# Two edits in an eight-sequence decoder kernel: output products of the first self attention per pair of sequences' halves, and the tail of the second self attention in another order

## The reference, cut to what matters

```
x = x + L0_attn(layernorm(x))            # 16 heads of 64, relative bias, softmax, then out @ Wo + bo
x = x + L0_xattn(layernorm(x), ctx)      # cross attention
x = x + L0_ffn(layernorm(x))             # 16 gated experts
x = x + L1_attn(layernorm(x))            # below
x = x + L1_xattn(layernorm(x), ctx)
x = x + L1_ffn(layernorm(x))             # 8 experts

# L1_attn(z): attention, then two layer norms with gamma and beta
h   = layer_norm(z + attention(z) @ Wout + bout) * gamma + beta
ffn = relu(h @ W1 + b1) @ W2 + b2
out = layer_norm(h + ffn) * gamma + beta
```

## Time and profile before

| | us |
|---|---|
| median of 3 runs (581.82, 582.07, 584.65) | 582.07 |
| the profiled execution | 586.07 |
| its span, first to last instruction | 584.3 |
| first self attention's loop in it, from the first scores to the last addition to x_all | about 117 |
| tail of the second self attention in it, from L1659 to the last L1671 | 35 |
| PE busy in the span | 482.6 (83%) |
| DVE, ACT, POOL busy | 372.1, 335.4, 264.1 |

### The profile page before, as it was taken

One profiled execution on the slowest core, in us unless ns is written; L12 is line 12 of the kernel. 1 busy time (PEld: TensorE's weight loads), 2 busy tenths in 40 slices (PEclk: granted clock), 3 DMA queues, 4 the chain that ended last, 5 costly groups with the idle time before them and its releaser, 6 DMA issues. The chain is left out here.

```text
span 584.3 us, 10052 instructions
## 1 busy us (share of the span) xinstructions
PE 482.6 (83%) x3221; PEld 370.9 (63%) x3221; DVE 372.1 (64%) x906; ACT 335.4 (57%) x659; POOL 264.1 (45%) x294
## 2 busy tenths in 40 slices
PE   4699999998688858899986995927678687999996
PEld 2578787876466636688853674524456474777774
DVE  4777777764737635466654676377437467788875
ACT  3787676765447745355543452404447465888883
POOL 1799687767335640566643900012001471354410
PEclk9799999999759976999995998877779957999999
DMA  6605332333264000544414000002660001121101
GB/s 190 210 24 151 94 101 84 92 89 101 75 145 121 1 2 2 156 134 130 123 38 121 1 1 0 1 14 69 169 163 1 2 1 37 37 59 51 36 0 36
DMA packets 34689, 41.81 MB, mean 72 GB/s; under 512 B 5178, under 2 KB 26612, under 8 KB 34420
## 3 DMA queue, kind: packets, MB, share of 16 engines
q1 hardware_dynamic: 33796, 40.65, 25.2%
q10 hardware_dynamic: 848, 0.60, 0.4%
HBM read 30.70 MB, written 8.18 MB: 67 GB/s over the span
## 5 line engine op out<-in xcount | busy, mean ns | idle before, releaser
L1251 POOL TENSOR_TENSOR e_gc<-e_g,e_c 128x512 f32<-128x512 f32 x32 | 42.0, 1313 | 42.3 <-ACT e_g L1234 22.4
L1995 DVE TENSOR_TENSOR e_h_lo<-e_h,e_h_hi 128x512 fp32r<-128x512 f32 x60 | 51.0, 881 | 15.1 <-ACT e_h_hi L1856 15.0
L944 ACT ACTIVATE x_pT<-x_turn 77x1024 f32<-77x1024 f32 x32 | 32.6, 1020 | 33.4 <-PE x_turn L890 33.4
L1852 ACT ACTIVATE e_h<-e_h,m_b 128x512 f32<-128x512 f32 x64 | 43.5, 686 | 11.0 <-PE e_h L1754 10.9
L546 ACT ACTIVATE a_p<-xn_all,a_least 128x128 f32<-128x128 f32 x128 | 40.7, 390 | 6.1 <-DVE a_least L578 6.0
L890 PE MATMUL x_turn<-consts,x_p 128*77 128x128 f32 x256 | 40.1, 306 | 4.5 <-ACT x_p L949 4.5
L692 POOL TENSOR_TENSOR a_p<-a_p,a_r 128x512 f32<-128x512 f32 x32 | 33.3, 1040 | 20.1 <-DVE a_r L587 20.1
L890 PEld LDWEIGHTS x_turn<-consts,x_p 128*77 128x77 f32 x256 | 32.0, 165 | 14.2 <-ACT x_p L949 12.1
L1210 ACT ACTIVATE e_h_hi<-e_h 128x512 fp32r<-128x512 f32 x34 | 21.5, 632 | 33.8 <-DVE e_h L1293 28.2
L1299 DVE TENSOR_TENSOR e_h_lo<-e_h,e_h_hi 128x512 fp32r<-128x512 f32 x34 | 23.8, 699 | 26.3 <-ACT e_h_hi L1210 26.3
L575 DVE TENSOR_TENSOR xn_all<-a_score,w_bias 128x256 f32<-128x256 f32 x64 | 24.1, 419 | 23.0 <-PE a_score L445 23.0
(11 more groups left out here) (302 smaller groups left out, 1471.2 us busy)
## 6 DMA issues: line engine op xcount, KB each, us to landing
e_c<-spread SPq DMA_DIRECT2D x32, 256.0 KB, 3.3
x_ks<-kstack SPq DMA_DIRECT2D x16, 462.0 KB, 5.7
kstack<-a_blk_hi SPq DMA_DIRECT2D x32, 154.0 KB, 3.1
m_w<-in_L_ffn_W SPq DMA_DIRECT2D x16, 256.0 KB, 3.0
a_raw<-in_experts SPq DMA_DIRECT2D x17, 192.0 KB, 2.4
kstack<-a_blk_lo SPq DMA_DIRECT2D x16, 154.0 KB, 2.8
su_reversed<-scratch SPq DMA_DIRECT2D x1, 1024.0 KB, 5.9
w_wkv<-in_L_attn_Wkv SPq DMA_DIRECT2D x1, 1024.0 KB, 8.1
```

The lines of the kernel that those rows point to most:

```text
L944: act.activation(pT[k % 2][:, :, :], tb[0:NKV, :, :], ACT.Copy).then_inc(S["turned_out"], 1)
L1251: pool.tensor_tensor(gc[k % 2][:, :], g[u % 2][:, :], c[k % NC][:, :], ALU.mult).then_inc(S["weighted"], 1)
L1852: act.activation(h[half][f], hb[f][:, :], ACT.Gelu, bias=b1[j][:, f:f + 1]).then_inc(S["gelu_done"], 1)
L1995: dve.tensor_tensor(h_lo[half][f][:, :], h[half][f], h_hi[half][f][:, :].bitcast(F32), ALU.subtract).then_inc(S["lo_done"], 1)
```

## The change

In attention0 the output products are made in odd t alone, for both sequences of a pair at once, with the operands the other way round: the weights are stationary and 256 columns (two sequences of 128 positions) move, so the result comes out transposed. After every eighth group ACT copies it to SBUF (yT), PE transposes it back into the other half of the same bank, and DVE adds from there to x_all, one step later than before and at the start of its step. In the second self attention a norm is four statistics, four aggregates and the variance as before, then four instructions (y - mean) * gamma, which don't need POOL's result, then four y * rstd + beta, each with a semaphore of its own for the transposes; in the last norms the addition of x_all takes the place of the one of beta. The separate passes L1652, L1663 and L1671 are gone. PE's order is turn(0), up(0), turn(1), down(0), up(1), down(1).

```diff
-                for n in range(G + OUT):
+                for n in range(G + OUT + 1):
...
+                    t = n - OUT - 1
+                    if 0 <= t < G and t % 8 == 7:
+                        pe.wait_ge(S["yT_out"], t // 8 + 1)
+                        for k in range(2):
+                            mm = pe.transpose(yb[:, 2 + k, :], yT[:, P * k:P * k + P], ident)
+                        mm.then_inc(S["y_turned"], 1)
                     t = n - OUT
-                    if 0 <= t < G:
-                        i, hg, b = t // 8, (t // 2) % 4, t % 2
-                        if t == 0:
+                    if 0 <= t < G and t % 2 == 1:
+                        i, hg = t // 8, (t // 2) % 4
+                        if t == 1:
...
                         for c in (2 * hg, 2 * hg + 1):
-                            mm = pe.matmul(yb[:, b, :], oT[:, b, c, :], wo[:, c, :], start=(c == 0 and b == 0),
-                                           stop=(c == 7 and b == 1))
+                            mm = pe.matmul(yb[:, 0:2, :], wo[:, c, :], oT[:, :, c, :], start=(c == 0), stop=(c == 7))
...
-                for n in range(G + VALUE):
+                for n in range(G + OUT + 1):
+                    t = n - OUT - 1
+                    if 0 <= t < G and t % 8 == 7:
+                        act.wait_ge(S["y_done"], 4 * (t // 8) + 4)
+                        act.activation(yT[:, :], yb[:, 0:2, :].rearrange("p b d -> p (b d)"),
+                                       ACT.Copy).then_inc(S["yT_out"], 1)
...
-                for n in range(G + OUT + 1):
+                for n in range(G + OUT + 2):
+                    t = n - OUT - 2
+                    if 0 <= t < G and t % 8 == 7:
+                        i = t // 8
+                        dve.wait_ge(S["y_turned"], i + 1)
+                        dve.wait_ge(S["bo_added"], 1)
+                        xp = x_all[:, 2 * i:2 * i + 2, :]
+                        dve.tensor_tensor(xp, yb[:, 2:4, :], xp, ALU.add).then_inc(S["x_out"], 1)
...
-                    t = n - OUT - 1
-                    if 0 <= t < G and t % 8 == 7:
-                        i = t // 8
-                        dve.wait_ge(S["y_done"], t + 1)
-                        dve.wait_ge(S["bo_added"], 1)
-                        xp = x_all[:, 2 * i:2 * i + 2, :]
-                        dve.tensor_tensor(xp, yb[:, 0:2, :], xp, ALU.add).then_inc(S["x_out"], 1)
...
-                def norm(k, h):
+                def norm(k, h, dst, add, done):
...
+                    own_values(*[dve.scalar_tensor_tensor(out=y[:, b, :], in0=y[:, b, :], scalar=mv[:, b, 0:1], in1=gamma,
+                                                          op0=ALU.subtract, op1=ALU.mult) for b in of_half])
                     dve.wait_ge(S["rstd_ready"], k + 1)
-                    own_values(*[dve.tensor_scalar(y[:, b, :], y[:, b, :], mv[:, b, 0:1], rstd[:, b:b + 1],
-                                                   ALU.subtract, ALU.mult) for b in of_half])
-                    own_values(dve.tensor_tensor(ys[h], ys[h], free(gamma, [[0, HB], [1, P]]), ALU.mult))
+                    for b in of_half:
+                        dve.scalar_tensor_tensor(out=dst[:, b, :], in0=y[:, b, :], scalar=rstd[:, b:b + 1], in1=add(b),
+                                                 op0=ALU.mult, op1=ALU.add).then_inc(done, 1)
...
-                    norm(h, h)
-                    dve.tensor_tensor(hs[h], ys[h], free(beta, [[0, HB], [1, P]]), ALU.add).then_inc(S["h_ready"], 1)
+                    norm(h, h, hh, lambda b: beta, S["h_ready"])
...
-                    norm(2 + h, h)
-                    own_values(dve.tensor_tensor(xs[h], xs[h], ys[h], ALU.add))
+                    norm(2 + h, h, x_all, lambda b: x_all[:, b, :], S["x_ready"])
```

More of the change, by code:

```diff
@@ L345, in attention0 @@
             oT = sb("oT", [P, 2, 8, P])
+            yT = sb("yT", [P, PT2])
             raw = [sb(f"raw{j}", [P, 3 * P]) for j in range(2)]
@@ L356, in attention0 @@
                      "scores_done", "biased", "max_done", "exp_done", "sum_done", "recip_done", "normed", "turn_done",
-                     "turned_out", "pv_done", "oT_out", "y_done", "x_out", "bo_added", "k_split", "blk_hi_done",
+                     "turned_out", "pv_done", "oT_out", "y_done", "yT_out", "y_turned", "x_out", "bo_added", "k_split", "blk_hi_done",
                      "blk_lo_done", "blk_hi_stored", "blk_lo_stored", "ld", "cast", "one_set", "landed0", "landed1",
@@ L591, in _ @@
                         if t >= 8:
-                            dve.wait_ge(S["y_done"], t - 7)
+                            dve.wait_ge(S["y_done"], t // 2 - 3)
                         hg, b = (t // 2) % 4, t % 2
                         dve.tensor_copy(oT[:, b, 2 * hg:2 * hg + 2, :], ob[:, 0:2, :]).then_inc(S["oT_out"], 1)
-                    t = n - OUT - 1
-                    if 0 <= t < G and t % 8 == 7:
-                        i = t // 8
-                        dve.wait_ge(S["y_done"], t + 1)
-                        dve.wait_ge(S["bo_added"], 1)
-                        xp = x_all[:, 2 * i:2 * i + 2, :]
-                        dve.tensor_tensor(xp, yb[:, 0:2, :], xp, ALU.add).then_inc(S["x_out"], 1)
                     if n == 0:
@@ L1399, in attention1 @@
                      "oT_done", "oT_out", "y_done", "step", "var_ready", "rstd_ready", "h_ready", "hT_done", "hT_out",
-                     "up_done", "relu_done", "down_done", "pick_landed", "pick_cast")
+                     "up_done", "relu_done", "down_done", "x_ready", "pick_landed", "pick_cast")
             S = {n: sem(n) for n in names}
@@ L1487, in _, with turn, up @@
                               wout[:, :], start=True, stop=True).then_inc(S["y_done"], 1)
-                for h in range(2):
-                    pe.wait_ge(S["h_ready"], h + 1)
+                def turn(h):
                     for b in range(HB * h, HB * h + HB):
+                        pe.wait_ge(S["h_ready"], b + 1)
                         mm = pe.transpose(tb[h][:, b % HB, :], hh[:, b, :], ident)
                     mm.then_inc(S["hT_done"], 1)
+                def up(h):
                     pe.wait_ge(S["hT_out"], h + 1)
@@ L1499, in _, with down @@
                                   start=True, stop=True).then_inc(S["up_done"], 1)
-                for h in range(2):
+                def down(h):
                     for b in range(HB * h, HB * h + HB):
@@ L1506, in _ @@
                     mm.then_inc(S["down_done"], 1)
+                turn(0)
+                up(0)
+                turn(1)
+                down(0)
+                up(1)
+                down(1)
             @block.scalar
@@ L1661, in _ @@
                 for h in range(2):
-                    norm(h, h)
-                    dve.tensor_tensor(hs[h], ys[h], free(beta, [[0, HB], [1, P]]), ALU.add).then_inc(S["h_ready"], 1)
-                dve.wait_ge(S["h_ready"], 2)
+                    norm(h, h, hh, lambda b: beta, S["h_ready"])
+                dve.wait_ge(S["h_ready"], B)
                 own_values(*[dve.tensor_tensor(ns[h], hs[h], free(b2, [[0, HB], [1, P]]), ALU.add) for h in range(2)],
```

## The result

| us | before | after |
|---|---|---|
| median | 581.95 (580.88 to 584.65, 4 runs) | 567.74 (567.44 to 568.49, 4 runs) |
| the profiled execution | 586.07 | 567.44 |
| its span | 584.3 | 565.7 |

The ratio of the two is 0.9751, 95% interval 0.9716 to 0.9786: the change makes the kernel 14.2 us faster, against 13.0 forecast and a time of 569.1.

The account below looks back on a forecast made before the run. PE's own instructions were taken to bound attention0's loop, and one serial chain across engines the second self attention's tail. Gains of 6.2 + 6.8 = 13.0 us took the median from 582.07 to 569.1, range 565.9 to 572.6.

Parts of the forecast that it names:

- part 1: Attention0's output product edits: a gain of 4.8 + 3.8 - 0.9 - 1.5 = 6.2 us, bounds 2.5 and 9.
- part 2: Second self attention's tail, fused norms and reordered products: a gain of 6.8 us, bounds 4.7 and 8.6.
- the price of a record: Attention0's output products: 0.143 us per 128 columns, 0.215 per 256, 0.07 per group change; a gain of 4.8 us.
- The transposes: PE's added transposes in attention0's loop: 0.3 us for two records, three times, a loss of 0.9 (0.3 to 1.5).
- The waits: Attention0's loop: PE's three waits for DVE's addition to x_all go, all of 3.8 us gained.
- The loop's end: After attention0's last fills: a longer last chain, with 0.1 for uneven steps, loses 1.5 us (0.9 to 2.2).
- the sign of 2.3: Second self attention's tail: first transposes were to come near 2.3 us after the variance.
- 1, no overlap of small instructions: Tail's norms: small DVE instructions don't overlap, 1.1 us less gain, 570.2 in all; chance 0.14.
- 2, short steps that don't shrink: Attention0's loop: odd steps stay near 3.2 us, 3.5 lost instead of 4.8 gained, 577.4 in all; chance 0.08.
- 3, a late clock: Tail: clock rises late and the relu stall is larger, 5.0 us gained instead of 6.8, 570.9 in all; chance 0.08.
- 4, a clock below 1.00 in the loop: Attention0's loop: new waits lower the granted clock, 5 us lost per stretch, four such giving 589; chance 0.02.
- 5: Both edits: the chain to x_out is as late as before and the norms' path doesn't end last, about 580; chance 0.03.

Follow-up runs that it names:

- the second set: The runs of e1 to e4 with 17 runs of the kernel before (median 582.84); the changed kernel's ratio there was 0.9782.
- e2: Kernel before with only the second self attention's fused norms and PE's new order; 575.11 us, ratio 0.9867.
- e5: Kernel before with only PE's new order in the second self attention's tail, norms as before; 579.55 us, ratio 0.9967.
- e6: Kernel before with only the fused norms in the second self attention's tail, PE's order as before; 579.82 us, ratio 0.9968.
- e1: Kernel before with only the attention0 edits (paired wide output products, copy, transposes, later addition), tail as before; 577.36 us, ratio 0.9913.
- e4: The changed kernel once more, no further edit, beside other runs on the same chip; 570.13 us, ratio 0.9782 against the kernel before.
- e11: The changed kernel a third time, no further edit, a single execution; 567.76 us.
- e7: Kernel before with only DVE's addition to x_all moved from the end to the start of its step; 579.09 us, ratio 0.9947.
- e8: e3 with one redundant wait on PE added in each even t; 569.66 us, ratio 0.9791 against the kernel before.
- e3: Changed kernel, but attention0's paired output products as eight 128-column records, without copy or transposes, addition where it was before; 570.18 us, ratio 0.981 against before.

## Why the prediction was right, point by point

**The window and the direction** were right: 567.7 against 569.1, inside 565.9 to 572.6. The two edited stretches gave 4.5 + 7.3 = 11.8, forecast 13.0. The measured 14.2 (and 12.7 in the second set) lies above that. Part of it may be the long wait at the end of the first stage, which two of three traces of before had (1.4 to 1.6 us more; two of six with e2, e5 and e6) and none of the four with the whole of part 1 (after, e1, e4, e11); the rest fits within the variation of stages that nobody touched. A forecast of 13.0 thus came out close partly by luck: part 1 gave 1.7 less than told and part 2 0.5 more, and the rest came from things that the forecast didn't contain.

**The term that was mis-sized: the price of a record.** I divided a span of eight records by seven, after taking off a guess of 0.30 for the drain, got 0.143 for 128 columns and so had only 0.07 left for the change of group. The split that the runs show is 0.11 and 0.2: those eight records of the earlier trace rows are the output products of two groups, so the fixed part stands once inside that span. My prices gave the right total for four records of 128 (0.64, from the row itself), and 0.215 for a record of 256 was right, but with 0.07 in place of 0.2 the group of four came to 0.93, where 1.06 was measured. So 25 x 0.64 - 12 x 1.06 = 3.3 us, not 4.8. The section of the Trainium skill that I called on (TensorE: Matmul & The Clock Gate, Back-to-back issue gap: short matmuls pay for their loads) finds no support here, and my "the trace agrees" was wrong: the records of 128 columns, each with a weight load of its own, followed each other in 0.11 us, half the time of 256. What is paid once, 0.2, belongs to the group.

**The transposes** cost 0.37 for the two, not 0.3: 1.1 in the loop, not 0.9. Same cause.

**The waits** went entirely, 3.9. Sum of the loop: 3.3 + 3.9 - 1.1 = 6.1; the length from step 5's scores to step 30's fell from 92.2 to 86.4, 5.8. The missing 0.3 is near a new wait of 0.4 of the probabilities' transposes (L456) for POOL between 40 and 50 us, early in the loop, which before didn't have.

**The loop's end** lost 1.7 up to the last addition (17.49 against 15.80 from step 30's scores; I had 1.5), of which 0.4 came back because the barrier now follows the addition after 0.30, where before it waited 0.68 for the stores. The stage ended 1.3 later for it. That SP's wait would "cover a little of the loss" was right. So part 1 is 5.8 - 1.3 = 4.5, not 6.2. The waits, the shorter odd steps and the longer end stood as told; the saving by the wider form did not, and the waits' 3.9 needed neither pairs nor transposes, as e7 shows.

**Part 2** gave 7.3, forecast 6.8 (its own ends, 391.89 and 385.0, give 6.9). Four of the new instructions take 1.13 to 1.14, as told, and the idle time between DVE's two halves was 2.74 (forecast 2.7). The product with W1 began 3.75 after the variance instruction (357.35 - 353.60) where before it was 5.71 (365.29 - 359.58): 2.0 gained, forecast 2.1. The first transpose began 1.80 after it (355.40 - 353.60); the sign of 2.3 that I had named for it didn't come, and isn't what the sum had used. What part 2 gave beyond the forecast is the clock: I left up(0) at 6.0 until the next group, and it took 362.65 - 357.35 = 5.3. Of that 0.7, some 0.2 went again where down(1) took 4.11 against 3.74 for down(0), a stall of 0.4 in place of 0.2. Windows of both kernels (columns as above, PEclk behind the counts):

```profile
361.00:365.00 4.00, 1.11 (x4) 0.71 (x4) 3.71 (x15) 0.36 (x1) 0.08 (x1) 0.50 0.00 0
365.00:369.00 4.00, 3.71 (x5) 1.64 (x6) 2.94 (x7) 0.93 (x2) 0.93 (x1) 0.50 0.00 0
```

```profile
357.00:361.00 4.00, 3.65 (x5) 1.58 (x6) 3.75 (x15) 0.99 (x2) 1.04 (x1) 0.51 0.00 0
361.00:365.00 4.00, 4.00 (x27) 3.00 (x26) 1.43 (x3) 2.55 (x4) 0.00 (x0) 1.00 0.00 0
```

Before (first fence), 1.2 GHz held up to about 370.2, 4.9 us after up(0) had begun; in the changed kernel (second) up to about 361, 3.6 after. PE had been idle for 3.95 us before the transposes there, not 6.07. All thirteen traces fall into these two groups: with the old norms the clock rose 4.7 to 5.1 us after up(0) had begun, with the new ones 3.1 to 3.6. I had bounded this on both sides and kept before's length.

**The rivals.** 1, no overlap of small instructions: out, by the 1.13 for four. The section of the Trainium skill that spoke for it (VectorE: DVE Perf Modes, The TRN2 errata) would have counted for it only if small ones didn't overlap at all: one takes 0.35, four 1.13, so they start 0.26 apart. What the section says of many small tiles the trace bears out: four of 128 columns take 1.13 where one of 512 takes 0.743. 2, short steps that don't shrink: out, 2.53. 3, a late clock: the other way. 4, a clock below 1.00 in the loop: out, 1.00. 5: out. None of them had the wait for the stores at the stage's end as something that varies, by 1.5 us.

**What stays open.** That the code packet causes the long wait is not shown: it is there in three of three and absent in ten of ten, and the redundant waits of e8 moved both, but no run moved the packet alone. Nor is it shown what moves the granted clock in the untouched stages. But that their length, 186 to 192 us behind the tail, goes with that clock, the traces do show. The stages after the tail in the first and the third execution of before:

```profile
392.35:584.30 191.95, 159.03 (x953) 120.43 (x953) 129.98 (x250) 124.53 (x214) 58.94 (x54) 0.88 0.20 51
```

```profile
394.13:580.60 186.47, 155.45 (x953) 118.07 (x953) 129.85 (x250) 124.23 (x214) 58.95 (x54) 0.89 0.21 53
```

PE is busy 3.6 us longer in the first; DVE, ACT and POOL are as busy in both within 0.3. By the clock's records 1.2 GHz was granted for 45.2 and 39.7 us of these. Over all thirteen traces, six of 185.7 to 186.7 us had it for 38.9 to 39.9 us, five of 188.8 to 189.6 for 42.0 to 42.8, and the two of 190.8 and 191.9 for 47.5 and 45.2; kernels with and without the change stand in each of the three groups but the last, which has before and e6. In the first cross attention, 71 to 74 us long in all traces, the clock differs as well. Windows of that stage, which the change leaves alone, in before and then in the changed kernel:

```profile
145.08:218.82 73.74, 54.87 (x500) 39.72 (x500) 42.03 (x113) 39.91 (x66) 34.52 (x35) 0.82 0.28 69
```

```profile
141.03:213.25 72.22, 53.16 (x500) 37.94 (x500) 41.96 (x113) 40.03 (x66) 34.59 (x35) 0.84 0.28 70
```

## What to carry over

Before a product is given another shape, look for the wait beside it: one moved addition brought 3.9 of the 4.5 us of a part that also added copies and transposes, and pairs in the old form (e8) had a stage 1.5 us shorter than the change's. Price a group of matmuls as a fixed part plus its columns, and get the two from two groups of different length in the loop itself. And where an effect of a few us sits in one stage, compare that stage's length over several traces and keep a second trace of the kernel before: two medians and two spans mix it with stages that vary by as much.

## What the runs showed of the hardware that I had not expected

- An f32 record of the output products at a clock of 1.00 took 0.11 us for 128 columns and 0.21 for 256, and a group of four or eight of them a fixed 0.2 beside (before, after, e3). The two transposes' group, 0.37, leaves 0.15 for it. A redundant wait where no group stands cost nothing (e8: odd steps 2.53).
- The same program, the kernel before, spent 186.5 to 191.9 us in the stages after the tail, with 1.2 GHz granted for 39.7 and 45.2 us of them.
- Four f32 instructions of 128 x 128 with a scalar and a second operand took 1.13 us on DVE, one 0.35, and one of 128 x 512 took 0.743.
- The last stores of the first stage landed 2.2 to 2.3 or 3.7 to 3.8 us after SP had begun to wait for them, with nothing between, and in all three long cases a packet of instructions was under way beside them.
